# Edge sum with four gathered lists and three block lists per group, and the repeated one-hot operands kept in PSUM

## The reference, cut to what matters

```python
xn = _layernorm(x, axis=-1)                      # 6250 x 256
# edges: src, dst of 200000 edges, sorted by dst; w = edge_weight
gathered = w[:, None] * xn[dst]
gnn = segment_sum(gathered, src, num_segments=6250) + node_vec1
x = x + gnn + linear_attention(xn)               # L0_mix weights
x = x + top2_of_8_experts(_layernorm(x))         # L0_ffn weights
```

## Time and profile before

| | |
|---|---|
| median of three runs | 2285.66 us (2284.79 to 2289.71) |
| span of the profiled execution | 2536.7 us |
| around its span | nothing is recorded, so its own time is taken as its span |
| busy in that span | PE 88%, PEld 76%, DVE 77%, ACT 46%, POOL 61% |
| gathers of the edge sum | 1029, busy 1143.9 us |
| mean granted clock of PE | 0.929 |

### The profile page before, as it was taken

How to read it: one execution, slowest core, us unless ns; L and a number is a source line. 1 busy time by engine, 2 the same in 40 slices (tenths; PEclk the granted TensorE clock), 3 DMA queues, 4 the chain that set the end, 5 groups by cost and what they waited for, 6 DMA issues and landing times. The chain is left out here.

```text
span 2536.7 us, 45539 instructions
## 1 busy us (share of the span) xinstructions
PE 2230.1 (88%) x16549; PEld 1930.5 (76%) x16550; DVE 1963.9 (77%) x3350; ACT 1174.3 (46%) x1696; POOL 1551.1 (61%) x1356
## 2 busy tenths in 40 slices
PE   7987799999999899989988998999989944999993
PEld 4656687777887788778877787778877844999993
DVE  7989888788898788878877897879877757555552
ACT  2236544443444344434443454444322235888772
POOL 4750266666676566666665666666766612778883
PEclk9989999999999899989988999999999977999997
DMA  5532422222223222222222222222244453455555
GB/s 151 150 113 87 123 82 75 76 90 78 74 83 90 73 82 76 88 76 80 76 82 73 83 79 84 78 79 77 82 123 139 136 180 61 79 81 83 82 81 133
DMA packets 160931, 235.90 MB, mean 93 GB/s; under 512 B 54834, under 2 KB 121805, under 8 KB 160490
## 3 DMA queue, kind: packets, MB, share of 16 engines
q0 software_dynamic: 70896, 164.43, 25.4%
q1 hardware_dynamic: 75536, 55.29, 7.9%
q10 hardware_dynamic: 14314, 13.68, 1.6%
HBM read 186.46 MB, written 53.24 MB: 94 GB/s over the span
## 5 line engine op out<-in xcount | busy, mean ns | idle before, releaser
L817 POOL DMA_INDIRECT picked<-xn_dram,place x1029 | 1143.9, 1112 | 721.7 <-PE bank L915 289.8
L1027 ACT COPY stage<-bank 128x512 f32<-128x512 f32 x343 | 201.0, 586 | 796.9 <-remote 477.6
L915 PE MATMUL bank<-picked,pick_w 128*128 128x256 f32 x2058 | 518.4, 389 | 3.3 <-issue 3.3
L915 PEld LDWEIGHTS bank<-picked,pick_w 128*128 128x128 f32 x2058 | 405.7, 197 | 65.8 <-issue 5.2
L911 PE MATMUL bank<-window,stage 128*128 128x256 f32 x1568 | 416.9, 409 | 17.8 <-issue 12.8
L903 PE MATMUL bank<-hot_w,hots 128*128 128x128 bf16 x4116 | 312.0, 225 | 49.1 <-issue 44.8
L911 PEld LDWEIGHTS bank<-window,stage 128*128 128x128 f32 x1568 | 300.4, 202 | 65.1 <-issue 25.6
L1164 DVE TENSOR_TENSOR vals<-hot_t,field_rep 128x1666 bf16<-128x1666 bf16 x200 | 203.7, 1041 | 187.8 <-remote 180.2
L1288 DVE TENSOR_TENSOR hot_w<-hots,cur 128x1536 bf16<-128x1536 bf16 x343 | 328.6, 958 | 11.9
L903 PEld LDWEIGHTS bank<-hot_w,hots 128*128 128x128 bf16 x4116 | 267.1, 101 | 92.5 <-issue 54.5
L911 PE MATMUL bank<-stage 128*128 128x256 f32 x1176 | 315.5, 410 | 11.6 <-issue 10.4
(11 more groups left out here) (253 smaller groups left out, 3414.6 us busy)
## 6 DMA issues: line engine op xcount, KB each, us to landing
picked<-xn_dram,place POOLq DMA_INDIRECT x1029
w<-in_L_ffn_W_dram SPq DMA_DIRECT2D x16, 512.0 KB, 8.9
xn_dram<-xn ACTq DMA_DIRECT2D x49, 128.0 KB, 1.9
xT_dram<-xT ACTq DMA_DIRECT2D x49, 128.0 KB, 2.1
base_dram<-acc SPq DMA_DIRECT2D x7, 896.0 KB
sum_dram<-acc SPq DMA_DIRECT2D x7, 896.0 KB
z_dram<-vals SPq DMA_DIRECT2D x7, 896.0 KB
out_dram<-sum_dram SPq DMA_DIRECT2D x1, 6250.0 KB, 21.8
```

The lines of the kernel that those rows point to most:

```text
L817: pool.indirect_dma_start(out=picked[:, i % SETS * PICK + q, :], out_offset=None, in_=xn_dram, in_offset=bass.IndirectOffsetOnAxis(ap=plac ...
L915: mm = pe.matmul(sum_ps[pp], pick_w[i % SETS][:, q, :], picked[:, i % SETS * PICK + q, :], start=False, stop=(q == PICK - 1))
L1027: act.copy(block_sb[pp].rearrange("p j c -> p (j c)"), banks[pp][:, :]).then_inc(a_copied, 1)
```

## The change

The change swaps the roles: read tiles 1, 3, 5 of a group are now blocks (`DENSE` 3), tiles 0, 2, 4, 6 are gathered (`PICK` 4). The repeated copies have 8 values in place of 16 (`REP`), and lie in PSUM banks 2 and 3, one bank for each half of a unit, with one buffer in place of two: a half is written again when its last tile's `hots` and `picks` are done. ACT copies table words of two bf16 values as one fp32 word, so the table holds each value twice (`[P, ROWS, NB, 2]`). The window loads tiles 1, 3, 5; the row numbers in `place` are clamped at 0; the order of list making follows the new roles; the attention's PSUM banks move from 2, 3 to 4, 5.

```diff
-REP = 16
+REP = 8
...
-    DENSE, PICK = (GRP + 1) // 2, GRP // 2
+    DENSE, PICK = GRP // 2, (GRP + 1) // 2
...
-        table = [sb(f"table{i}", [P, NB, ROWS], BF16) for i in range(2)]
+        table = [sb(f"table{i}", [P, ROWS, NB, 2], BF16) for i in range(2)]
...
-        cur = [sb(f"cur{i}", [P, BU, ROWS, REP], BF16) for i in range(2)]
-        cur_w = [sb(f"cur_w{i}", [P, BU, PICK, REP]) for i in range(2)]
...
+        CUT = (0, 4, BU)
+        CUR_W = CUT[1] * ROWS * (REP // 2)
...
+        def cur_words(half):
+
+            return banks[2 + half][:, 0:(CUT[half + 1] - CUT[half]) * ROWS * (REP // 2)]
+
+        def cur_w(half):
+
+            return banks[2 + half][:, CUR_W:CUR_W + (CUT[half + 1] - CUT[half]) * PICK * REP]
...
-                sp.dma_start(window[g % 2][:, :, :], rows[:, 0:GRP:2, :]).then_inc(window_in[g % 2], 16)
+                sp.dma_start(window[g % 2][:, :, :], rows[:, 1:GRP:2, :]).then_inc(window_in[g % 2], 16)
...
+            def take(used, par, k, half):
+
+
+                act.wait_ge(w_done, used + 1)
+                act.wait_ge(pick_done, used + 1)
+                a, n = k * BU + CUT[half], CUT[half + 1] - CUT[half]
+                act.copy(cur_w(half).rearrange("p (m r) -> p m r", r=REP),
+                         weight[par][:, a:a + n, :].rearrange("p i q -> p (i q)").unsqueeze(2).broadcast_to([P, n * PICK, REP]))
+                words = table[par][:, :, :, :].rearrange("p f b h -> p (f b h)").bitcast(F32).rearrange("p (f b) -> p b f", b=NB)
+                act.copy(cur_words(half).rearrange("p (i f r) -> p i f r", f=ROWS, r=REP // 2),
+                         words[:, a:a + n, :].unsqueeze(3).broadcast_to([P, n, ROWS, REP // 2])).then_inc(cur_done, 1)
...
-                act.copy(block_sb[pp].rearrange("p j c -> p (j c)"), banks[pp][:, :]).then_inc(a_copied, 1)
+                act.copy(block_sb[pp].rearrange("p j c -> p (j c)"), banks[pp][:, 0:DENSE * P]).then_inc(a_copied, 1)
...
-                dve.tensor_tensor(place[par][:, bass.ds(q, 1), :].rearrange("p a b -> p (a b)"), row[:, :],
-                                  first_row[:, bass.ds(s, 1)].broadcast_to([P, NB]), ALU.add)
+                dve.tensor_scalar(place[par][:, bass.ds(q, 1), :].rearrange("p a b -> p (a b)"), row[:, :],
+                                  first_row[:, bass.ds(s, 1)], 0.0, ALU.add, ALU.max)
```

More of the change, by code:

```diff
@@ L678, in edge_sum @@
         before_each = bass.AP(tile_pad, 0, [[2 * WIDE, P], [2, CH // 2], [WIDE, 2], [1, CH]])
+        hot_w = [w[:, :, 0:DENSE, :] for w in hot_w]
         def block_ps(par, j):
@@ L700, in xT_part @@
             return picked[:, i, k * P:(k + 1) * P] if c % 2 else stage[:, i * D + k * P:i * D + (k + 1) * P]
-        mix_ps = [banks[i][:, 0:D] for i in range(4)]
+        mix_ps = [banks[i][:, 0:D] for i in (0, 1, 4, 5)]
         kv_ps = [banks[4][:, c * D:c * D + P + 2] for c in range(2)]
@@ L1044, in begin @@
                 act.wait_ge(listed, 3 * PICK)
-                take(0, 0, 0, 0, 0)
-                take(0, 0, 0, 0, 1)
+                take(0, 0, 0, 0)
+                take(0, 0, 0, 1)
                 evacuate(0, 0)
@@ L1072, in unit @@
                         repeat_fields(s, 3, FIELDS)
-                    if after and i in (2, 4):
+                    if after and i in (CUT[1] - 1, CUT[2] - 1):
                         if turned:
@@ L1169, in part @@
                 dve.wait_ge(unpacked, s + 1)
-                bits = table[par][:, :, :].bitcast(U16)
-                both, dst = (bits[:, :, at:at + DENSE][:, :, bass.ds(j, 1)].rearrange("p b a -> p (a b)") for at in (AT_SRC, PICK))
+                both, dst = (table[par][:, at + j, :, :].rearrange("p b h -> p (b h)").bitcast(U16) for at in (AT_SRC, PICK))
                 dve.tensor_scalar(dst, both, 0x7F80, None, ALU.bitwise_and)
@@ L1273, in sort, with hots @@
                 if s % 2 == 1:
-                    part(s - 1, (s - 1) // 2, 0)
+                    make_list(s - 1, s // 2, s // 2, 0)
                 elif s > 0:
-                    make_list(s - 1, s // 2 - 1, s // 2 - 1, 0)
-            def hots(t, i, odd, free):
+                    part(s - 1, s // 2 - 1, 0)
+            def hots(t, i, free):
                 if free is not None:
                     dve.wait_ge(a_done, free)
-                of = cur[odd]
+                of = cur_of(i)
                 to = hot[i % SETS]
@@ L1302, in begin @@
                 dve.wait_ge(cur_done, 2)
-                hots(0, 0, 0, None)
-                picks(0, 0, 0)
-                hots(1, 1, 0, None)
+                hots(0, 0, None)
+                picks(0, 0)
+                hots(1, 1, None)
                 dve.wait_ge(saved, 16 * GRP)
@@ L1323, in unit @@
                     if i + 1 < BU:
-                        picks(t + i + 1, i + 1, odd)
+                        picks(t + i + 1, i + 1)
                     elif after:
-                        picks(t + BU, 0, 1 - odd)
+                        picks(t + BU, 0)
                     if i == 2:
@@ L1329, in unit @@
                     if i + 2 < BU:
-                        hots(t + i + 2, i + 2, odd, t + i + 2 if i + 2 < 3 else t + i + 1)
+                        hots(t + i + 2, i + 2, t + i + 2 if i + 2 < 3 else t + i + 1)
                     elif after:
@@ L1333, in unit @@
                             dve.wait_ge(cur_done, 2 * (u + 1) + 1)
-                        hots(t + i + 2, i + 2 - BU, 1 - odd, t + i + 2)
+                        hots(t + i + 2, i + 2 - BU, t + i + 2)
                     if i > 0:
```

52 lines of the change are left out of this document (25 added, 27 removed).

## The result

The changed kernel takes 2613.3 us (median of four runs, 2607.04 to 2618.27), the kernel before 2287.26 us beside it (2284.79 to 2289.71, four runs). The ratio is 1.142, with a 95% interval from 1.1396 to 1.1443: slower by 326 us. The profiled execution of the changed kernel has a span of 2614.2 us and took 2616.2.

What follows compares the result with a forecast made beforehand. PE was taken to bound the kernel before; after the change POOL's gathers would, 1372 x 1.31 = 1797 us from 298.5, tiles ending at 2100 against 1800: 2285.7 + (2100 - 1800) = 2585 us, range 2430 to 2720.

Steps and rivals of the forecast that it cites:

- What bounds the kernel now: Edge-sum loop before the change: PE bounds at 4.37 us a tile, POOL close second at 4.25; loop ends at 1800.
- The pauses: Idle stretches behind each base in the edge sum, 270 us, taken to belong to the profiled execution, not ordinary runs.
- The sum for ordinary runs: Whole kernel: 2285.7 + (2100 - 1800) = 2585 us, from the shift of the end of the tiles.
- PE's part: Block matmuls on PE: three fewer save 0.17 us a tile, 58 us over 343 tiles, leaving 4.20 a tile.
- The gather: POOL, 343 gathers more: each 0.94 + 0.306 gap + 0.064 remaining disturbance = 1.31 us, 5.24 us a tile, above PE's 4.20.
- The first gather: Start of POOL's gathers: waits for the eighth sort step's list, so about 298.5 in place of 289.3.
- DVE, ACT, SP: Other engines in the loop: DVE falls from 4.26 to 4.10 us a tile, hidden behind POOL; ACT and SP cost nothing.
- PE's clock: PE in the tiles: 80% busy; even at a granted clock of 0.88 its 4.8 us a tile still fits.
- A: POOL's 0.306 us gap is absent outside the profile, gathers cost 1.00 us, PE stays bound: 2228 us; chance 0.14.
- B: DVE loses its bf16 rate on PSUM operands, `hots` 1.48 us, a tile 5.38 us: 2633 us; chance 0.10.
- C: Moving operands to PSUM frees nothing on POOL, a gather stays at 1.418 us: 2734 us; chance 0.08.

Runs made afterwards that it cites:

- the extra gather: Kernel before with PSUM operands, 8 repeats, single buffers and its old roles, plus a fourth gather a tile into a buffer nothing reads: 2609.0 us, ratio 1.141.
- the gather left out: Changed kernel without the fourth gather of each tile from the fifth tile on; its matmul uses old rows: 2247.93 us, ratio 0.9828.
- the repeat: The kernel before, run and profiled once more with no edit: 2284.47 us, profiled span 2282.7 us.
- the first experiment: Kernel before with the repeated operands in PSUM, 8 repeats and one buffer, keeping four block lists and three gathered: 2258.47 us, ratio 0.9871.
- the SBUF version: Changed kernel with its repeated operands in SBUF in place of PSUM, same layout and single buffer, four gathered lists: 2714.28 us, ratio 1.1872.

## Why the prediction was right, step by step

The forecast was 2585 us (range 2430 to 2720), measured were 2613.3. Its mechanism, POOL's gathers take PE's place as the bound, is shown by the extra gather and by the gather left out.

- **What bounds the kernel now: wrong in its order, right in its length.** The step took PE for the bound at 4.37 us a tile and POOL for a close second, at 4.25. In the repeated profile the tiles end at 1801.0, and the forecast had 1800. But a gather costs (1185.9 + 300.8) / 1029 = 1.445 us there, not 1.418, which is 4.33 us a tile, and with its waits for PE 4.39: POOL bound at least as much as PE, whose tile by itself is 4.27 us (1200 / 281 in the first experiment). The profile shown before had shorter gathers (a mean of 1.112 us against 1.152) because of its pauses: by my count 185 of its 1029 gathers began while DVE ran nothing, against 66 in the repeat. So the reading "the 289.8 us of waiting are about the size of the pauses, so they are no reserve" was right and should have been carried further: without pauses nothing is left of them.
- **The pauses: right that they don't belong to ordinary runs, wrong about whose they are.** The prediction gave them to the profiled execution, and then let its span stay near the ordinary time after the change on account of PE's slack. The repeat shows that profiling does not bring them; they were that one execution's. What made them isn't known. The sum for ordinary runs doesn't hang on it, since it started from 2285.7.
- **PE's part: right in sign and place.** With three block lists and one gather left out, PE had a tile of 4.22 us (1200 / 284) against 4.27 with four block lists, 0.05 less where 0.17 was forecast. It also waited 31 us for rows there, 0.09 a tile, which makes up most of the rest. It has no weight in the result: PE had 1 us a tile of slack.
- **The gather: the mechanism right, the size 1.31 where 1.328 was measured.** That is the mis-sized term. The base (0.94) and the gap (413.7 / 1358 = 0.305) came out as taken; the part that remains of the disturbance was forecast at 0.064 and is 1.023 - 0.94 = 0.083 us. The term had two faults. The 0.17 us of disturbance to start from came from the profile with the pauses; without them it is 1.152 - 0.94 = 0.21, and 37% of that is 0.078. And DVE's busy time is not the right measure: a gather loses the rest of the operation in which it began, so long operations count for more than their share, and where the gathers fall in them counts too. By my count of the excess over 0.945 us, `hots`, `hot_w` and `picks` cause 133 of 214 us in the repeat of before, and all the others 81, 0.078 us a gather. In the changed kernel the three cause none; `vals` causes 42 of 108 us, the three operations that write `earlier` 23, `hot_t` 17, `slot` 13 and `same` 10. The same operations left 0.070 us a gather in the first experiment and 0.146 with the fourth gather left out. So that the forecast came within 0.02 us is in part luck.
- **The first gather: 304.7 against 298.5.** The list work of the eighth step ends at 303.8. The SBUF version and the other descendants of the changed kernel began between 297.8 and 301.4, so at least 3 of the 6 us may be this execution's own. The end of the tiles came at 2133 against 2100: 25 for the gathers (1822 against 1797), 6 for the start, 1 or 2 for the last matmuls. The rest of the kernel was some 5 us shorter than the forecast took it to be, which leaves the 28.
- **DVE, ACT, SP: hidden, as forecast.** `hots`, `hot_w`, `picks` 814, 754 and 680 ns against 810, 740 and 690. DVE was busy 928 of 1200 us, with 243 us of waits for PE. The view of ACT's waits lists none for DVE in the stretch. The DMA share is 34%, against 36 forecast; the 27% that it was worked out from belong to the profile with the pauses, and the repeat has 33.
- **PE's clock:** the granted clock is 0.98 in the stretch and 0.957 over the span, no lower than the prediction allowed.
- **The rivals.** A (a gather without its gap, 2228 us) fell: the gap is in ordinary time, since 1372 gathers with it fill a loop that fits the ordinary time. B (2633 us) lies a little nearer to the measured time than the forecast, 20 us on the other side, and only the rows tell them apart: `hots` took 0.81 us, not 1.48. C (2734 us) is what the SBUF version shows, nearly: 2714.
- **The rules of the Trainium skill.** Of the gathers, the trace shows 0.94 us beside operations with one PSUM operand and 1.70 beside `vals`, with two in SBUF, and the move to SBUF costs 101 us. The Trainium skill (SBUF — State Buffer, "Who interferes with whom") says that a DVE instruction with two SBUF inputs contends with a GpSimd instruction that reads SBUF, and these runs agree. Of the DVE rate, `hots` takes 814 ns with an operand in PSUM and 816 without. The Trainium skill (VectorE: DVE Perf Modes, "The perf-mode tier table") has `tensor_tensor` at 1x for any PSUM operand, and the measurement decides against it here. The Trainium skill under "Why PSUM operands drop a tier" on the same page allows the rate that was measured.

A weak place of the prediction was to treat the two parts of the change as one sum. Apart, they are -28 us for the PSUM operands and, on top of them, +355 for one more gathered list (2613.3 - 2258.5).

## What to carry to other kernels

Here a gather cost the engine that issued it 1.2 us or more with its gap, however few its bytes. Count such DMAs, with the gaps that the busy share leaves out, before a list is moved from an engine that is full to one that looks two thirds busy. PE and POOL were both full before, and one part of the change made POOL's gathers cheaper while the other gave it a third more of them: 28 us won, 355 lost. Take such parts apart and keep the one that only relieves. A profile whose span is far longer than the median of the runs should be distrusted in its waits and its means: they can hide that a second engine is full.

## What the runs showed of the hardware

- A gather of 128 rows of 1 KB holds POOL for 0.94 us with nothing beside it, and a gap of 0.30 us stands ahead of the next. 512-byte rows take the same (median 0.945); 64 rows take 0.90 (median 0.902). Little of the price goes with the rows, and none that these runs can tell with the bytes.
- A gather that begins inside a DVE operation on two SBUF tiles ends about 0.82 us after that operation (549 of 591 in the repeat of before, within 0.80 to 0.83); a gather takes 0.945 us by itself. One that begins in the operation's first 0.02 us takes 0.945. So `vals`, 1.04 us long, made single gathers last up to 1.81 us. By my count in that trace, gathers begun in `hot_w` had a mean of 1.49 us, in `vals` 1.44, in `picks` 1.14 and in `hots` 1.02. `hots` costs little because of the phase: half of its gathers begin more than 0.73 us into its 0.88, those of `hot_w` 0.29 us into its 0.96.
- Of the 583 gathers of the changed kernel that began with more than 0.15 us left of an operation with an operand in PSUM, all but one (the first of the loop, 1.21 us) took 0.94 to 0.97 us.
- A bf16 `tensor_tensor` of 1280 elements took 814 ns with one operand in PSUM and 816 ns with both in SBUF.
- The same kernel had one profiled execution of 2536.7 us with pauses behind the bases in which ACT stood idle for up to 12.4 us, and one of 2282.7 without. What made the first stays open.
- With the fourth gather left out the other three were hindered more (1.091 us, against 1.015 in the kernel with the PSUM operands and the old roles). By my count of the excess, `hot_t` and `slot` cost it 35 us each, where they cost the changed kernel 17 and 13. That is phase again: in both kernels nearly all gathers begun in these two operations follow the rule above, but here the median one in `slot` began 0.31 us into it and there 0.85, and 42 began in `hot_t` against 29.
